# An SSM and mixture-of-experts kernel: GpSimd's skip, residual and low rows in other units, group 2's rows ahead of a weight split, group 3's projection in halves

## Chip, cores, metric

One NeuronCore of one Trainium2 chip. The time is the device time of one launch in microseconds (us); the profile is of one further execution.

## What is computed

The input `x` is 2 sequences of 2048 tokens of 256 numbers. First a state space layer, then a layer norm, then a mixture of experts, and a last layer norm; cut to its core:

```python
state = tanh(state @ A.T + x_t @ B.T)                 # 128 states, token after token
y  = states @ C.T + D * x + x
x1 = layernorm(x + layernorm(y) * gamma + beta)       # 256 numbers a token
scores = sigmoid(x1 @ router_weight.T)                # 8 experts in 2 groups of 4
# the better group (sum of its top two of scores + bias), in it the top 2 experts, weights normalised
routed = sum_e comb[t, e] * (silu(x1 @ w_gate[e]) * (x1 @ w_up[e])) @ w_down[e]
shared = (silu(x1 @ sw_gate) * (x1 @ sw_up)) @ sw_down
out = layernorm(x1 + routed + shared)
```

## The kernel before

**Data and stages.** The 4096 tokens lie as 32 tiles of 128 in `xres`; four tiles are a group, so there are 8 groups, 0 to 7. The scan runs all chunks of the sequences side by side in 64 steps; in the second 32 it leaves the states of one tile per step. Work on the first groups is put between those steps.

Every group goes through a *front*, each step on the engine that is named:

- GpSimd (`rows_in`): `skip` writes (D+1) * x into `xskip` (L1329), `residual` adds beta into `xres` (L1334), both 128x1024 in fp32.
- TensorE `project` (L385): states times C, eight matmuls into two PSUM banks, one for each half of two tiles; `c_done` counts the halves.
- VectorE `rows_sums` (L1009: PSUM plus `xskip`, a half each) and `row_moments` (L991 to L995), `scale_rows` (L1025), `sum_rows` (L1035), `sum_moments`: two layer norms. GpSimd takes the powers in `deviations1` (L1352, L1354) and `deviations2` (L1359 to L1365). ScalarE `normalise` (L710) writes the rows.
- ScalarE `high_rows` (L717) rounds the rows to fp16, and GpSimd `low_rows` (L1379) writes the rest as a second fp16 part; `note_tiles` (L1390) copies tile numbers.
- TensorE `turn_x2` (L396), ScalarE `keep_turned` (L724), TensorE `logits` (L403), ScalarE `scores` (a tanh, L733).
- VectorE `choose_group` (L1056 to L1072: nine instructions on 32 numbers a partition or fewer), TensorE `places` (L412 to L414), VectorE `sort_tiles` (L1135 to L1147), `choose_two` (L1086 to L1093), `weigh` (L1107 to L1119).
- TensorE `permute` (L418) with ScalarE `put` (L752), TensorE `turn_comb` (L438) with ScalarE `put_comb` (L761): tokens and weights sorted by expert group, at column offsets that VectorE casts to integers (L1147) and ScalarE reads (`offsets`).

**Passes and units.** The sorted tokens are taken in 10 passes, 0 to 9, of 2, 2, then six times 4, then 2, 2 tiles. A pass goes through 5 units (the shared expert, unit 0, and four routed ones), the last through 9: 54 units, n = 0 to 53. "Short" passes have 2 tiles, "wide" ones 4. A unit on TensorE is `up` (gate and up, L457), `spread` of the expert's weights (L467, which waits until the product before it is done), and two units later `down` (L480). ScalarE applies `silu` (L768) and rounds the product (`high`, L777); VectorE `inner` multiplies (L1155, or L1158 and L1162); GpSimd `low` (L1384) writes the product's low fp16 part, for which `down` waits. At a pass's end ScalarE `sums` and VectorE `close` (moments), GpSimd `deviations3`, ScalarE `finish` (L791), and GpSimd `send` (L1428: an indirect DMA for each tile).

**Order.** Every engine's queue is written out by hand and runs in order. In the loop over units each engine does its part of unit n and then the front steps that are due in it: `due(n, ahead, first)` gives the group whose position is `ahead` units on. So in a wide pass i the routing of group i + 1 and the rows of group i + 2 are under way: `choose_group` and `rows` in unit 0, `sort_tiles`, `scale_rows` and `sum_rows` in unit 1, `sum_moments` and `choose_two` in unit 2, `weigh` in unit 3. GpSimd's loop begins with

```python
for n, (i, j) in enumerate(UNITS):
    if n:
        low(n - 1, ...)
    g = due(n, EP, 2)                 # unit 0 of a wide pass
    if g is not None:
        low_rows(g, g % 3, main)
        note_tiles(g, main)
    ...                               # deviations1, plan, deviations2, watch, deviations3
    if 1 <= i <= G - 5 and j == 4:
        rows_in(i + 4)                # skip and residual of group i + 4
    if j in (0, 1) and i >= 2:
        send(i - 2, ...)              # half of pass i - 2's tiles
```

The weights are split into two fp16 parts by VectorE (`split`, L966 and L968, 128x2304): gate and up before the fronts, the down weights (`split(2)`) behind group 1's moments.

Of the kernel before, what the change touches and what calls it, by code (L numbers as in the profile page):

```python
# [20 lines left out]
def ssm_moe_kernel(nc, x, A, B, C, D, gamma, beta, router_weight, correction_bias,  # L21
# [20 lines left out]
    with ExitStack() as ctx:  # L42
# [181 lines left out]
        def ps_projected(g, half, sems):  # L224
            if sems is main and g == 2:
                return bank[half]
            return ps_misc[1 - half]
# [104 lines left out]
        def _(pe):  # L332
# [46 lines left out]
            def project(g, at, sems):  # L379

                for half in range(2):
                    if half and sems is main and g >= 3:
                        pe.wait_ge(main.th_done, g if g > 3 else 2)
# [140 lines left out]
            for i in range(L):  # L524
# [14 lines left out]
                if i == 24:  # L539
                    logits(0, main)  # L540
                if i == 27:
                    places(0)
                if i == 28:
                    pe.wait_ge(main.th_done, 1)
                    turn_x2(1, 1, main)
# [7 lines left out]
            project(3, 3 * T4, main)  # L553
# [53 lines left out]
            def front_late(n):  # L607
                g = due(n, EP + 2, 2)
# [87 lines left out]
        def _(act):  # L696
# [113 lines left out]
            for i in range(L):  # L810
# [6 lines left out]
                if i == 27:  # L817
                    high_rows(0, 0, main)
                if i == 25:
                    scores(0, main)  # L820
                if 23 <= i < 23 + T4:
                    normalise(1, 1, main, (i - 23,))
                if 28 <= i < 28 + T4:
                    at += offsets(0, (i - 28,))
                if i == 29:
                    keep_turned(1, main)

            put(0, 0, at)
# [87 lines left out]
        def _(dve):  # L916
# [80 lines left out]
            def rows_sums(g, par, sems):  # L997

                for half in range(2):
# [177 lines left out]
            for g in range(2):  # L1177
# [3 lines left out]
                sum_moments(g, g, main)  # L1181
            split(2)
            choose_group(0, main)
            sort_tiles(0)
            rows_sums(2, 2, main)
            choose_two(0, main)
            weigh(0, main)
            row_moments(2, 2, main)
            choose_group(1, main)
            scale_rows(2, 2, main)  # L1190
            rows_sums(3, 0, main)
            sort_tiles(1)

            for n, (i, j) in enumerate(UNITS):
# [28 lines left out]
                if n == 0:  # L1223
                    sum_moments(2, 2, main)
                if n == 2:
# [58 lines left out]
        def _(pool):  # L1284
# [52 lines left out]
            def rows_in(n):  # L1337
# [3 lines left out]
                skip(n)  # L1341
                pool.wait_ge(skip_done, (n + 1) * T4)
# [93 lines left out]
            note_tiles(0, main)  # L1436
            plan(0)
            watch(0)
            deviations1(2, 2, main)
# [3 lines left out]
            for n, (i, j) in enumerate(UNITS):  # L1443
                if n:
                    low(n - 1, n - 1, TILES[UNITS[n - 1][0]] * P, main)
                g = due(n, EP, 2)
                if g is not None:
                    low_rows(g, g % 3, main)
                    note_tiles(g, main)
# [4 lines left out]
                if g is not None:  # L1454
                    plan(g)
                g = due(n, 2 * EP - 2, 4)
# [11 lines left out]
                if j == 4 and i:  # L1468
                    deviations3(i - 1, (i - 1) % 2, TB[i - 1], TILES[i - 1], main)
                if 1 <= i <= G - 5 and j == 4:  # L1470
# [63 lines left out]
```

## Time and profile before

| what | value |
|---|---|
| median of 3 runs | 345.87 us (345.06 to 346.21) |
| the profiled execution | 347.44 us, span 345.7 us |
| TensorE matmul busy (PE) | 301.0 us, 87% of the span |
| VectorE busy (DVE) | 232.4 us, 67% |
| ScalarE busy (ACT) | 187.7 us, 54% |
| GpSimd busy (POOL) | 215.0 us, 62% |
| the chain that ended last, by engine | PE 38%, DVE 31%, issue 8%, POOL 7%, SP's queue 6%, ACT 5% |

The span is from the first to the last instruction of the profiled execution, and the rest of its time lies around it. Engine names in rows: PE is TensorE, DVE VectorE, ACT ScalarE, POOL GpSimd. A timeline row is: start and duration in us, engine, line, operation, what it writes and reads (by the buffers' names; several tensors share one, so that `low_rows` shows as `wg<-xskip,wg` and `low` as `h<-wu,h`), shape, how many of them the row merges, and in brackets the idle time of the engine just before and what ended it. A windows row has the window and its us, then busy us (instructions) of PE, of PE's weight loads, of DVE, ACT and POOL, then the granted TensorE clock as a share of full speed, the DMA share and GB/s.

### The profile page before, as it was taken

To read this page: it belongs to the slowest core of one execution; us is meant where nothing else is said; L and a number is where in the kernel's file an instruction comes from. 1 tells how busy PE (TensorE), PEld (TensorE's weight loads), DVE (VectorE), ACT (ScalarE), POOL (GpSimd) and SP (SyncE) were. 2 spreads that over 40 slices of the span, in tenths; PEclk is the share of its full clock that TensorE was granted. 3 is DMA by queue.
4 is the path that set the end of the run, shared out by engine and by line. 5 is a ranking of instruction groups with operands and counts; after the bars stand their busy time and mean duration, and the time that the engine had idled before them with its cause. 6 is when DMAs were issued, how large, how long until landed. Compare 5 with 4: busy or idle time off the path is not lost.

```text
span 345.7 us, 7383 instructions
## 1 busy us (share of the span) xinstructions
PE 301.0 (87%) x2255; PEld 228.7 (66%) x2255; DVE 232.4 (67%) x671; ACT 187.7 (54%) x442; POOL 215.0 (62%) x326
## 2 busy tenths in 40 slices
PE   5999999979878698798988999799999999998930
PEld 4998988878667465455655745476666656887820
DVE  2244979676998848995899599779936725363420
ACT  2465423545784593268358646756866772644430
POOL 8799013552545549567885986579777474776632
PEclk9999999985889999899999999999999999999985
DMA  6993000000000000000000010010001010011000
GB/s 190 339 335 121 0 3 0 0 2 0 2 2 2 0 2 1 33 0 2 15 19 1 2 43 20 0 34 32 0 17 48 2 47 15 28 37 63 30 8 32
DMA packets 6811, 13.20 MB, mean 38 GB/s; under 512 B 1000, under 2 KB 3568, under 8 KB 6768
## 3 DMA queue, kind: packets, MB, share of 16 engines
q1 hardware_dynamic: 5232, 8.47, 7.6%
q0 software_dynamic: 1536, 4.20, 3.4%
q8 instruction: 22, 0.36, 0.4%
q14 instruction: 21, 0.17, 0.2%
HBM read 8.47 MB, written 4.19 MB: 37 GB/s over the span
## 4 chain that ended last, share of the span: by engine, by line
PE 38%; DVE 31%; issue 8%; POOL 7%; SPq 6%; ACT 5%; DMA 2%; ACTq 1%; POOLq 0%; DVEq 0%
PE bank L457 14%; PE bank L480 8%; DVE st L991 5%; PE bank L403 4%; SPq L301 3%; DVE xskip L1035 3%; DVE xskip L1025 3%; PE bank L367 3%; DVE wd L1158 2%; DMA xres<-in_L_attn_x_dram 2%; PE bank L373 2%; POOL out_dram L1428 2%; DVE wu L1162 2%; DVE xskip L1009 2%; DVE more L1060 2%
## 5 line engine op out<-in xcount | busy, mean ns | idle before, releaser
L1384 POOL TENSOR_TENSOR h<-wu,h 128x512 f16<-128x512 f32 (+1 forms) x54 | 51.4, 953 | 50.9 <-ACT h L777 50.5
L480 PE MATMUL bank<-wd,h 128*128 (+1 forms) x504 | 65.2, 276 | 2.3 <-POOL h L1384 2.0
L457 PE MATMUL bank<-xT,wg 128*128 x324 | 64.6, 336 | 0.2 <-ACT wg L768 0.2
L457 PE MATMUL bank<-xT,wu 128*128 x324 | 63.4, 332 | 0.0
L768 ACT ACTIVATE wg<-bank,g_un 128x512 f32<-128x512 f32 (+1 forms) x54 | 31.9, 592 | 47.7 <-PE bank L457 47.5
L480 PEld LDWEIGHTS bank<-wd,h 128*128 128x128 f16 x504 | 47.8, 100 | 10.5 <-POOL h L1384 2.6
L1158 DVE SCALAR_TENSOR_TENSOR wd<-bank,u_un,wg 128x512 f32<-128x512 f32 (+1 forms) x44 | 27.2, 619 | 34.5 <-PE bank L457 17.8
L457 PEld LDWEIGHTS bank<-xT,wu 128*128 (+1 forms) x324 | 31.7, 98 | 23.0 <-issue 0.2
L457 PEld LDWEIGHTS bank<-xT,wg 128*128 (+1 forms) x324 | 31.3, 99 | 18.0 <-issue 1.1
L367 PE MATMUL bank<-xT,BT 128*128 128x128 f32 x256 | 41.4, 286 | 0.0
L752 ACT ACTIVATE xT<-bank 128x512 f32 (+1 forms) x64 | 33.8, 605 | 13.8 <-PE bank L418 9.4
L367 PEld LDWEIGHTS bank<-xT,BT 128*128 128x128 f32 x256 | 35.8, 202 | 0.1
L777 ACT ACTIVATE h<-wu 128x512 f16<-128x512 f32 (+1 forms) x54 | 28.6, 529 | 5.2 <-DVE wu L1162 4.5
L1162 DVE TENSOR_TENSOR wu<-bank,wd 128x512 f32<-128x512 f32 (+1 forms) x44 | 25.1, 570 | 1.5
L1379 POOL TENSOR_TENSOR wg<-xskip,wg 128x1024 f16<-128x1024 f32 x8 | 17.6, 2198 | 9.5 <-ACT wg L717 9.5
L991 DVE BATCH_NORM_STATS2 st<-xskip 128x6 f32<-128x256 f32 x64 | 22.4, 412 | 0.3
L1428 POOL DMA_INDIRECT out_dram<-z_odd,row_id x16 | 18.4, 1147 | 5.7 <-issue 3.2
L704 ACT ACTIVATE states<-bank 128x128 f32<-128x128 f32 x32 | 8.9, 277 | 22.2 <-PE bank L373 18.6
L1329 POOL TENSOR_TENSOR xskip<-xres,D_bc 128x1024 f32<-128x1024 f32 x8 | 18.9, 2358 | 1.6 <-PE bank L356 1.6
L710 ACT ACTIVATE xskip<-xskip,shift,rstd 128x256 f32<-128x256 f32 x32 | 17.2, 597 | 4.3 <-POOL shift L1365 4.3
L1334 POOL TENSOR_TENSOR xres<-xres,beta_bc 128x1024 f32<-128x1024 f32 x8 | 18.8, 2356 | 1.1
L704 ACT ACTIVATE run_state<-bank 128x128 f32<-128x128 f32 x31 | 8.6, 277 | 20.1 <-PE bank L373 20.1
(186 smaller groups left out, 568.2 us busy)
## 6 DMA issues: line engine op xcount, KB each, us to landing
xres<-in_L_attn_x_dram SPq DMA_DIRECT2D x7, 512.0 KB, 6.3
wd<-in_L_ffn_w_down_dram SPq DMA_DIRECT2D x1, 1024.0 KB, 6.7
xres<-in_L_attn_x_dram SPq DMA_DIRECT2D x2, 256.0 KB, 3.2
out_dram<-wd,row_id POOLq DMA_INDIRECT x16
out_dram<-z_odd,row_id POOLq DMA_INDIRECT x16
states<-in_L_attn_B_dram SPq DMA_DIRECT2D x1, 128.0 KB, 2.1
D_bc<-in_L_attn_D_dram SPq DMA_DIRECT2D x1, 128.0 KB, 5.0
beta_bc<-in_L_attn_beta_dram SPq DMA_DIRECT2D x1, 128.0 KB, 6.5
```

The source lines that it names most:

```text
L367: pe.matmul(ps_scan[s % 2][:, 0:P], BT[:, k, :], xT[:, k, tile, :], start=(k == 0), stop=False)
L457: last = pe.matmul(ps[:, 0:w], up_rows[which][pw][:, part], x2_sorted[:, k * 2 + px, bass.ds(col, w)], start=first, stop=(k == KT - 1 and ...
L480: last = pe.matmul(ps_y[t // 2][:, (t % 2) * DM:(t % 2 + 1) * DM], h16[:, m % 3, ph, t * P:(t + 1) * P], down_rows[pw][:, rows], start=(fi ...
L752: nc.scalar.activation(x2_sorted[:, :, bass.ds(where, P)], ps_rows(g, t)[:, :].rearrange("p (a c) -> p a c", a=2 * KT), ACT.Copy).then_inc ...
L768: nc.scalar.activation(sg[:, m % 2, 0:w], ps_g[:, 0:w], ACT.Silu, scale=g_un[:, 0:1]).then_inc(sems.silu_done, 1)
L777: nc.scalar.activation(h16[:, m % 3, 0, 0:w], h[:, m % 2, 0:w], ACT.Copy).then_inc(sems.h_high, 1)
L991: nc.vector.bn_stats(st[:, st_k, t, :], src(t)).then_inc(st_sem, 1)
L1158: nc.vector.scalar_tensor_tensor(gu[:, m % 2, 0:w], ps_u[m % 2][:, 0:w], u_un[:, 1:2], sg[:, m % 2, 0:w], ALU.mult, ALU.mult).then_inc(sem ...
L1162: nc.vector.tensor_tensor(h[:, m % 2, 0:w], ps_comb[:, 0:w], gu[:, m % 2, 0:w], ALU.mult).then_inc(sems.h_done, 1)
L1329: nc.gpsimd.tensor_tensor(xskip[:, n * T4:(n + 1) * T4, :], xres[:, n * T4:(n + 1) * T4, :], D_bc[:, :].unsqueeze(1).to_broadcast([P, T4, ...
L1384: nc.gpsimd.tensor_tensor(h16[:, m % 3, 1, 0:w], h[:, m % 2, 0:w], h16[:, m % 3, 0, 0:w], ALU.subtract).then_inc(sems.h_low, 1)
L1428: nc.gpsimd.indirect_dma_start(out_rows, bass.IndirectOffsetOnAxis(row_id[:, ring, t:t + 1], 0), z2s[par][:, t, :], None, bounds_check=N - ...
```

## The change

It changes the order of instructions only; none is added or removed, and one PSUM bank is another.

- The scan: `logits(0)` goes from step 24 to 23, `places(0)` from 27 to 28, `turn_x2(1)` from 28 to 27; on ScalarE `high_rows(0)` from 27 to 21, `scores(0)` from 25 to 23, `keep_turned(1)` from 29 to 28, the offsets of group 0 from steps 28 to 31 to steps 30, 31 and behind the scan.
- VectorE does `rows(2)` (sums and moments) ahead of `split(2)`, and `scale_rows(2)` ahead of `choose_group(1)`.
- Group 3's projection leaves its place ahead of the first unit: its halves go behind units 0 and 1, both into bank `ps_y[1]`, which short passes don't use; the second waits for the sum of the first. VectorE sums them in units 1 and 2.
- GpSimd: `deviations1(2)` ahead of `plan(0)`; in the loop `low_rows` and `note_tiles` go behind the sends of the same unit; the skip of group i + 4 goes from unit 4 to unit 2 of passes 1 to 3, ahead of `deviations2`, and the residual stays in unit 4.

```diff
@@ ps_projected
+            if sems is main and g == 3:
+                return ps_y[1]
@@ TensorE
-            def project(g, at, sems):
-                for half in range(2):
-                    if half and sems is main and g >= 3:
-                        pe.wait_ge(main.th_done, g if g > 3 else 2)
+            def project(g, at, sems, halves=range(2)):
+                for half in halves:
+                    if half and sems is main and g == 3:
+                        pe.wait_ge(main.y1_done, 2 * g + 1)
+                    if half and sems is main and g > 3:
+                        pe.wait_ge(main.th_done, g)
...
-                if i == 24:
+                if i == 23:
                     logits(0, main)
+                if i == 28:
+                    places(0)
                 if i == 27:
-                    places(0)
-                if i == 28:
                     pe.wait_ge(main.th_done, 1)
                     turn_x2(1, 1, main)
...
             turn_comb(0)
-            project(3, 3 * T4, main)
             taken_at[0] = take(0)
             places(1)
...
             def front_late(n):
+                if n in (0, 1):
+                    project(3, 3 * T4, main, (n,))
@@ ScalarE
-                if i == 27:
+                if i == 21:
                     high_rows(0, 0, main)
-                if i == 25:
+                if i == 23:
                     scores(0, main)
...
-                if 28 <= i < 28 + T4:
-                    at += offsets(0, (i - 28,))
-                if i == 29:
+                if 30 <= i < 30 + T4:
+                    at += offsets(0, (i - 30,))
+                if i == 28:
                     keep_turned(1, main)
+            at += offsets(0, range(len(at), T4))
@@ VectorE
+            rows(2, 2, main)
             split(2)
             choose_group(0, main)
             sort_tiles(0)
-            rows_sums(2, 2, main)
             choose_two(0, main)
             weigh(0, main)
-            row_moments(2, 2, main)
+            scale_rows(2, 2, main)
             choose_group(1, main)
-            scale_rows(2, 2, main)
-            rows_sums(3, 0, main)
             sort_tiles(1)
...
+                if n == 1:
+                    rows_sums(3, 0, main, (0,))
+                if n == 2:
+                    rows_sums(3, 0, main, (1,))
@@ GpSimd
+            deviations1(2, 2, main)
             plan(0)
             watch(0)
-            deviations1(2, 2, main)
...
                     low(n - 1, n - 1, TILES[UNITS[n - 1][0]] * P, main)
-                g = due(n, EP, 2)
-                if g is not None:
-                    low_rows(g, g % 3, main)
-                    note_tiles(g, main)
...
                     plan(g)
+                if 1 <= i <= G - 5 and j == 2:
+                    pool.wait_ge(x_in[i + 4], 16)
+                    skip(i + 4)
...
                 if 1 <= i <= G - 5 and j == 4:
-                    rows_in(i + 4)
+                    rows_kept(i + 4)
                 if j in (0, 1) and i >= 2:
...
                     send(i - 2, i % 2, (i - 2) % 3, TB[i - 2], TILES[i - 2], main, range(j * half, (j + 1) * half))
+                g = due(n, EP, 2)
+                if g is not None:
+                    low_rows(g, g % 3, main)
+                    note_tiles(g, main)
```

## Rows read from the trace of the kernel before

**Rows 1.** Windows view, passes 2 to 5: busy us (instructions), clock, DMA.

```profile
130.00:163.10 33.10, 28.07 (x189) 17.53 (x189) 27.66 (x72) 17.58 (x38) 23.11 (x32) 0.95 0.03 9
163.10:193.80 30.70, 27.90 (x201) 18.07 (x200) 26.07 (x75) 18.39 (x39) 24.14 (x31) 1.00 0.03 10
193.80:225.30 31.50, 28.07 (x201) 18.15 (x201) 26.84 (x76) 19.56 (x41) 22.40 (x34) 1.00 0.05 18
225.30:253.20 27.90, 27.28 (x201) 18.24 (x200) 23.23 (x75) 19.14 (x41) 21.02 (x32) 1.00 0.06 20
```

**Rows 2.** Timeline, VectorE, pass 2: start, us, engine, line, operation, count, idle before.

```profile
131.95 1.70 DVE L1056 TENSOR_SCALAR score<-th 128x32 f32<-128x32 f32 x1 [1.16 <-ACT th L733]
...
134.31 2.04 DVE L1060 TENSOR_TENSOR more<-choice 128x16 f32<-128x16 f32 x1
...
139.24 1.29 DVE L1009 TENSOR_TENSOR xskip<-bank,xskip 128x512 f32<-128x512 f32 x2
```

**Rows 3.** Timeline, GpSimd (POOL), the same stretch.

```profile
131.25 2.35 POOL L1334 TENSOR_TENSOR xres<-xres,beta_bc 128x1024 f32<-128x1024 f32 x1
...
134.19 2.13 POOL L1379 TENSOR_TENSOR wg<-xskip,wg 128x1024 f16<-128x1024 f32 x1
```

**Rows 4.** Timeline, VectorE, the chain undisturbed, in pass 4, in pass 5.

```profile
84.74 0.18 DVE L1056 TENSOR_SCALAR score<-th 128x32 f32<-128x32 f32 x1 [2.14 <-ACT th L733]
...
86.24 1.67 DVE L1025 SCALAR_TENSOR_TENSOR xskip<-xskip,mv,gamma_bc 128x256 f32<-128x256 f32 x4
...
195.84 0.78 DVE L1056 TENSOR_SCALAR score<-th 128x32 f32<-128x32 f32 x1 [1.15 <-ACT th L733]
...
200.79 1.29 DVE L1009 TENSOR_TENSOR xskip<-bank,xskip 128x512 f32<-128x512 f32 x2
...
227.30 1.17 DVE L1056 TENSOR_SCALAR score<-th 128x32 f32<-128x32 f32 x1 [1.15 <-ACT th L733]
...
229.82 1.29 DVE L1009 TENSOR_TENSOR xskip<-bank,xskip 128x512 f32<-128x512 f32 x2
```

**Rows 5.** Timeline, VectorE, from the split to the first unit.

```profile
63.80 2.62 DVE L968 SCALAR_TENSOR_TENSOR wd<-wd,wscale 128x2304 f16<-128x2304 f32 x1
69.78 0.18 DVE L1056 TENSOR_SCALAR score<-th 128x32 f32<-128x32 f32 x1 [3.37 <-ACT th L733]
...
72.49 0.21 DVE L1135 TENSOR_TENSOR_SCAN zeros_f<-ones_row,zeros_f,bank 1x4 f32<-1x4 f32 x1 [1.24 <-PE bank L414]
...
73.80 2.09 DVE L1147 CAST zeros_i<-zeros_f 1x4 int32<-1x4 f32 x1
...
80.79 1.40 DVE L991 BATCH_NORM_STATS2 st<-xskip 128x6 f32<-128x256 f32 x4
...
90.71 0.46 DVE L1155 SCALAR_TENSOR_TENSOR wu<-bank,u_un,wg 128x256 f32<-128x256 f32 x1
```

**Rows 6.** Timeline, GpSimd, the first low_rows.

```profile
73.21 2.65 POOL L1379 TENSOR_TENSOR wg<-xskip,wg 128x1024 f16<-128x1024 f32 x1 [5.51 <-ACT wg L717]
```

**Rows 7.** Timeline, ScalarE (ACT), group 1's first normalisation.

```profile
67.74 0.60 ACT L710 ACTIVATE xskip<-xskip,shift,rstd 128x256 f32<-128x256 f32 x1 [2.12 <-POOL shift L1365]
```

**Rows 8.** Timeline, TensorE (PE), the projection ahead of the first unit.

```profile
84.71 3.73 PE L385 MATMUL bank<-CT,states 128*128 128x256 f32 x8
```

**Rows 9.** Timeline, GpSimd, short pass 1, pass 4, pass 5.

```profile
120.12 0.67 POOL L1384 TENSOR_TENSOR h<-wu,h 128x256 f16<-128x256 f32 x1 [1.69 <-ACT h L777]
...
214.58 0.20 POOL L1359 TENSOR_TENSOR rstd<-mv,eps 128x4 f32<-128x4 f32 x1 [2.88 <-DVE mv L995]
...
228.74 1.13 POOL L1428 DMA_INDIRECT out_dram<-z_odd,row_id  x1 [0.15 <-ACT z_odd L791]
```

**Rows 10.** Timeline, TensorE, the wait for the weights in pass 5.

```profile
247.63 0.40 PE L438 MATMUL bank<-perm,comb 128*128 128x128 f16 x4 [0.53 <-DVE comb L1119]
```

**Rows 11.** Timeline, VectorE, weigh in pass 1, scaling in pass 4.

```profile
121.13 0.19 DVE L1110 SCALAR_TENSOR_TENSOR kept<-rank,score 128x32 f32<-128x32 f32 x1
...
206.59 3.21 DVE L1025 SCALAR_TENSOR_TENSOR xskip<-xskip,mv,gamma_bc 128x256 f32<-128x256 f32 x4
```

More of the change, by code:

```diff
@@ L995, in stats, with rows_sums @@
                     nc.vector.bn_aggr(to[:, t, :], st[:, st_k, t, :]).then_inc(mv_sem, 1)
-            def rows_sums(g, par, sems):
-                for half in range(2):
+            def rows_sums(g, par, sems, halves=range(2)):
+                for half in halves:
                     dve.wait_ge(sems.c_done, g * 2 + half + 1)
@@ L1341, in rows_in, with rows_kept @@
                 skip(n)
+                rows_kept(n)
+            def rows_kept(n):
                 pool.wait_ge(skip_done, (n + 1) * T4)
```

## The prediction, on record before the change was run

> **What bounds the kernel now.** I read the windows view first, cut where VectorE notes a new wide pass (four tiles). TensorE is busy 28 us in each of passes 2, 3 and 4 and 27.3 us in pass 5, with the same work in all four; but pass 5 lasts 27.9 us and the others 33.1, 30.7 and 31.5 [rows 1]. So TensorE's work is a floor of about 27.3 us, and passes 2 to 4 stand 3 to 6 us above it.
>
> Next the VectorE timeline of the slowest pass. The routing chain `choose_group(3)` starts at 131.95, and the sums that follow it at 139.24: 7.3 us for nine tiny instructions, single ones of 1.70 and 2.04 us [rows 2]. The GpSimd timeline says why [rows 3]: a residual runs from 131.25 to 133.60, and L1056 ends at 133.65; `low_rows` runs from 134.19 to 136.32, and L1060 ends at 136.35. A VectorE instruction on SBUF that starts inside a large GpSimd instruction ends when that one ends. Undisturbed the same chain takes 84.74 to 86.24, that is 1.5 us; in pass 4 it takes 4.95 us (pass 3 is like it, 0.3 us shorter), in pass 5, which has no skip and residual ahead of it, 2.5 us [rows 4].
>
> The Trainium skill (SBUF — State Buffer, "Who interferes with whom") calls this an exclusive lock: VectorE and GpSimd share one pair of ports, held for a whole instruction. The rows above agree to 0.1 us.
>
> Last, the stretch from the end of the scan to the first unit. VectorE holds the split's second half from 63.80 to 66.42 and spends 2.09 us on a 1x4 cast at 73.80 [rows 5], inside `low_rows(0)` at 73.21 [rows 6]; ScalarE, which runs the scan's tanh in the same queue, waits for that cast's result, and before it 2.12 us for GpSimd's deviations, held up by the split [rows 7]. The projection of group 3 then takes 3.73 us ahead of the first unit [rows 8], whose VectorE work begins at 90.71 [rows 5].
>
> **The change, part by part.** T is the instant at which the tanh of a group's logits ends.
>
> *Group 2's rows ahead of the split, the scan's steps in another order.* I follow VectorE from `choose_group(0)` to the first unit. It starts about 1 us later: the rows (two sums of 0.65, moments 1.41, aggregates 0.4: 3.1 us) push the split into the 3.37 us in which VectorE waits [rows 5], and `low_rows(0)`, which `high_rows(0)` at step 21 now releases near the split, can hold that for up to its own 2.65 us [rows 6]. I take half. From there on the chain loses: the cast's lockout (2.09 - 0.15 = 1.95), group 2's sums (1.3), its moments (1.85), group 3's sums (1.3) and part of the 2.14 us wait for the tanh of group 1, which the scan, no longer standing 2.12 us and at the cast, brings earlier [rows 4, 5, 7]: 1.1, half. It gains the wait for `places(1)`, now with nothing beside it (group 0's is 1.24, I take 0.7 [rows 5]), and a lockout by `low_rows(1)`, which falls between `choose_group(1)` and `sort_tiles(1)` (0 to 2.13; half, 1.1). +1.0 - 1.95 - 1.3 - 1.85 - 1.3 - 1.1 + 0.7 + 1.1 = -4.7 us: the first unit near 86.0. Bounds: both lockouts in full and no earlier tanh, -1.2; none of them, -8. TensorE no longer has the projection's 3.73 us ahead of the unit, so it isn't what comes last.
>
> *Group 3 in halves.* TensorE's halves (under 1.9 us each) go behind units 0 and 1, where it waits for VectorE; the two sums go into VectorE's units 1 and 2. VectorE has no break there and carries `weigh(1)`, for which TensorE waits. One of the two stands ahead of it: +0.65 us (0 to 1.3).
>
> *The skip at unit 2, the residual alone at unit 4, `low_rows` behind the sends.* The residual now ends a skip earlier, about 1 us before T, and `low` near T. A send waits for `finish`, which ScalarE runs behind the tanh; its DMA takes 1.13 us [rows 9]. So `low_rows` starts some 2 us after T in passes 2 and 3 (one DMA) and 3.3 us in passes 4 and 5 (two), when `choose_group` (1.5 us) is over and VectorE is at sums, moments and the unit's products, which read PSUM or one operand: L1009 keeps 0.65 us apiece [rows 2]. So `choose_group` falls to 1.5 us: 5.8, 3.2, 3.45 and 1.0 us less in passes 2 to 5. TensorE's floor caps what comes of it.
>
> What is late next is the skip's new place. Behind it on GpSimd stand the second deviations and the next unit's `low`; ScalarE's normalisation waits for the first, TensorE's down projection for the second. A skip has the residual's shape and its 2.35 us [rows 3]. Two rows bound its price. In pass 4 GpSimd is idle 2.88 us, from 211.70 to the second deviations at 214.58 [rows 9]: there it would fit, price 0. But what ends that idle time is the moments, and right behind them on VectorE stands `choose_two`; that comes 18.8 us behind T now and, 3.45 us earlier, at T+15.3, while GpSimd is free near T+15.9 or, with less in its way, some 2 us before. So the skip meets `choose_two` or `weigh` in passes 2 and 3: 0 to 2.35 us of VectorE. TensorE waits for `weigh`'s result (already 0.53 us in pass 5 [rows 10]). I take 1.6 us: 27.4 + 1.6 = 29.0 us each (27.5 to 30). In pass 1 the skip starts when `low(6)` ends, 120.79 [rows 9], `weigh(2)`, for whose end TensorE waits, reads two SBUF operands from 121.13 on [rows 11]: 120.79 + 2.35 - 121.13 = +2.0 us (0 to 3). Passes 4 and 5 have no skip; what remains is `low` among the scaling: four of 3.21 us in pass 4 [rows 11] against 1.67 undisturbed [rows 4], so up to 1.5 us. I take 27.9 and 27.6 (27.3 to 28.8).
>
> The Trainium skill (same page and section) says that issue order decides who blocks, and that the other blocks fully. That speaks against this part: a skip is issued ahead of the routing on which TensorE waits next. By it each of the three skips costs 2.35 us, 7.05 in place of 5.2, and the sum below would be -9.9. L1060 agrees that the loser blocks fully; who comes first at the new place no row shows.
>
> **Sum.** First unit -4.7, halves +0.6, pass 1 +2.0, pass 2 from 33.1 to 29.0 = -4.1, pass 3 -1.7, pass 4 -3.6, pass 5 -0.3: -11.8 us. Passes 6 to 9 keep their work. The profiled execution took 347.44 us (span 345.7, the rest around it), 1.6 us above the median of the runs, 345.87; the difference carries over: 334.1 us.
>
> **Rivals.**
> 1. *Down to TensorE's floor.* The skips fall into GpSimd's idle time, pass 1 loses nothing, passes 2 to 5 take 27.4 or 27.5: 123.2 - 109.8 = -13.4, with -4.1 early -17.5: 328.4 us. For it: pass 5 is within 0.6 us of its floor. Against: the idle slot ends where `choose_two` starts.
> 2. *The skip locks out in full.* 2.35 us three times (+1.9), and each pushes `low` back, so that TensorE's down projection waits another 1 us (+3): -6.9, 339.0 us. For it: pass 1's rows. Against: VectorE can come first.
> 3. *Slower: the large operations only change their victim.* `low_rows` behind the sends reaches `sort_tiles` and the scaling, for which the permutation waits. It decides if it starts later than T+4.5: a DMA issue stretched by 1.2 us does it. Price per pass 2.13, and 1.55 for the `low` behind it, in four passes, plus three skips: 14.7 + 7.05 = 21.8, against 13.45 of stalls removed and 4.1 early: +4.2, 350 us. Against: the second DMA should end by T+3.3.
> 4. *It doesn't do what it says.* GpSimd is a microsecond late everywhere, residual and `low` still run into `choose_group`, and the skips cost as forecast: the passes give nothing, pass 1's skip takes 2.0 and one other 1.6 of the early 4.1: 345.4 us.
>
> **How the numbers follow.** Forecast 0.57, rival 1 0.20, rival 2 0.15, rival 3 0.05, rival 4 0.03. The forecast's own bounds are 330 to 338; the range reaches to rivals 1 and 2 and takes in the bounds of the first part: 327.5 to 341. A measurement of this kernel can tell 0.3% (1 us) from no change: faster 0.92, same 0.03, slower 0.05.
>
> **What would show it.** Right: L1060 at 0.2 us and 1.5 us for `choose_group` in passes 2 to 5, with `low_rows` behind the DMAs; windows of 28 to 29 us; the first L1155 near 86; ScalarE's stand of 2.12 us gone; a skip beside `choose_two` (L1086 to L1093) or `weigh` (L1110), with one of those at 1 to 2.4 us. Wrong: TensorE waiting for `low` (L1384) at its down projections; L1144 or L1025 stretched by `low_rows`; a first unit that starts no earlier, because `choose_group(0)` starts later.

## The result, and the profile after

The changed kernel takes 335.52 us (median of 4 runs, 332.56 to 337.0) against 345.65 us of the kernel before on the same chip: ratio 0.968, 95% interval [0.965, 0.972]. The forecast was 334.1 us, in a range of 327.5 to 341. Its profiled execution took 337.0 us (span 335.3), the longest of the four.

The line numbers of the changed kernel are 4 to 12 higher than before: `choose_group` L1063 to L1079, `rows_sums` L1016, `scale_rows` L1032, `sum_rows` L1042, `choose_two` L1093 to L1100, `weigh` L1114 to L1126, `skip` L1338, `residual` L1343, `low_rows` L1391, `low` L1396, `send` L1440; on TensorE `project` L389, `turn_comb` L442.

First the windows view of passes 2 to 5, cut as [rows 1]:

```profile
127.30:155.80 28.50, 26.49 (x194) 17.20 (x190) 22.84 (x71) 17.76 (x38) 21.87 (x33) 1.00 0.03 11
155.80:186.60 30.80, 28.94 (x201) 19.50 (x201) 24.08 (x75) 18.32 (x39) 23.32 (x32) 0.94 0.03 10
186.60:215.60 29.00, 27.54 (x201) 18.36 (x201) 23.66 (x76) 19.45 (x41) 19.36 (x32) 1.00 0.06 20
215.60:243.50 27.90, 27.33 (x201) 18.31 (x200) 22.53 (x76) 19.18 (x41) 20.47 (x32) 1.00 0.06 20
```

Pass 2 lost 4.8 us and pass 4 2.5, pass 5 nothing; pass 3 is as long as before. From one cast of the row numbers, with which VectorE opens a pass, to the next (us):

| | first unit | pass 0 | pass 1 | pass 2 | pass 3 | pass 4 | pass 5 | sum to pass 6 |
|---|---|---|---|---|---|---|---|---|
| before | 90.64 | 21.79 | 17.50 | 33.15 | 30.73 | 31.47 | 27.95 | 253.23 |
| after | 85.80 | 22.17 | 19.48 | 28.37 | 30.81 | 28.96 | 27.91 | 243.50 |
| difference | -4.84 | +0.38 | +1.98 | -4.78 | +0.08 | -2.51 | -0.04 | -9.73 |
| forecast | -4.7 | +0.6 | +2.0 | -4.1 | -1.7 | -3.6 | -0.3 | -11.8 |

*What went as forecast.* The VectorE timeline of pass 2, then the GpSimd timeline beside it (columns as in [rows 2, 3]):

```profile
129.47 0.18 DVE L1063 TENSOR_SCALAR score<-th 128x32 f32<-128x32 f32 x1 [1.16 <-ACT th L739]
129.92 0.17 DVE L1067 TENSOR_TENSOR more<-choice 128x16 f32<-128x16 f32 x1
130.97 1.36 DVE L1016 TENSOR_TENSOR xskip<-bank,xskip 128x512 f32<-128x512 f32 x2
```

```profile
124.98 2.35 POOL L1343 TENSOR_TENSOR xres<-xres,beta_bc 128x1024 f32<-128x1024 f32 x1
...
130.94 1.26 POOL L1440 DMA_INDIRECT out_dram<-wd,row_id  x1 [2.98 <-ACT wd L797]
132.24 2.14 POOL L1391 TENSOR_TENSOR wg<-xskip,wg 128x1024 f16<-128x1024 f32 x1
...
142.23 2.35 POOL L1338 TENSOR_TENSOR xskip<-xres,D_bc 128x1024 f32<-128x1024 f32 x1
145.14 0.20 POOL L1371 TENSOR_TENSOR rstd<-mv,eps 128x4 f32<-128x4 f32 x1 [0.56 <-DVE mv L1002]
```

The 7.3 us of [rows 2] are 1.5 us (129.47 to 130.97), and the instruction that took 2.04 us takes 0.17. The residual is over 2.1 us before `choose_group` starts, and `low_rows` starts 1.3 us after `choose_group` is done, behind a send. This skip cost nothing: it ends at 144.58, and GpSimd then still waits 0.56 us for the moments; without it, in experiment 5, the pass takes 28.38 us against 28.37.

*What the large operations hit next.* VectorE in passes 1, 2, 3 and 4; the first and third row stand in a skip (GpSimd, below), the second and fourth hold `low`:

```profile
116.69 2.01 DVE L1117 SCALAR_TENSOR_TENSOR kept<-rank,score 128x32 f32<-128x32 f32 x1
...
137.06 2.90 DVE L1032 SCALAR_TENSOR_TENSOR xskip<-xskip,mv,gamma_bc 128x256 f32<-128x256 f32 x3
...
172.36 2.18 DVE L1093 TENSOR_TENSOR choice<-choice,mask 128x32 f32<-128x32 f32 x1
...
198.48 3.20 DVE L1042 SCALAR_TENSOR_TENSOR xskip<-xskip,rstd,xres 128x256 f32<-128x256 f32 x4
```

```profile
116.30 2.35 POOL L1338 TENSOR_TENSOR xskip<-xres,D_bc 128x1024 f32<-128x1024 f32 x1
...
138.50 1.17 POOL L1396 TENSOR_TENSOR h<-wu,h 128x512 f16<-128x512 f32 x1
...
172.13 2.34 POOL L1338 TENSOR_TENSOR xskip<-xres,D_bc 128x1024 f32<-128x1024 f32 x1
...
198.67 1.14 POOL L1440 DMA_INDIRECT out_dram<-wd,row_id  x1 [0.31 <-issue]
199.80 1.19 POOL L1396 TENSOR_TENSOR h<-wu,h 128x512 f16<-128x512 f32 x1
```

L1117 takes 0.19 us where nothing is beside it, L1093 0.17. All four stand ahead of `weigh` or in it, and TensorE waits for `weigh` at the end of the pass. Its wait there in pass 1 of the kernel before, then in passes 1 to 5 of the changed one (timelines of TensorE):

```profile
122.69 0.40 PE L438 MATMUL bank<-perm,comb 128*128 128x128 f16 x4 [0.32 <-DVE comb L1119]
```

```profile
120.25 0.40 PE L442 MATMUL bank<-perm,comb 128*128 128x128 f16 x4 [2.33 <-DVE comb L1126]
...
150.29 0.40 PE L442 MATMUL bank<-perm,comb 128*128 128x128 f16 x4 [1.38 <-DVE comb L1126]
...
179.68 0.40 PE L442 MATMUL bank<-perm,comb 128*128 128x128 f16 x4 [1.39 <-DVE comb L1126]
...
210.05 0.40 PE L442 MATMUL bank<-perm,comb 128*128 128x128 f16 x4 [1.39 <-DVE comb L1126]
...
237.91 0.40 PE L442 MATMUL bank<-perm,comb 128*128 128x128 f16 x4 [0.49 <-DVE comb L1126]
```

In pass 1 the wait grew by 2.0 us. In passes 2 to 4 it was 1.38 to 1.39 us before too. So 1.39 says that VectorE is the later of the two at the end of a pass, but not by how much: TensorE's matmul just ahead waits for VectorE's last product, `weigh` follows that product without a break, and the remaining wait is then the same however late VectorE is. What a pass lost is read from its length.

*The early part.* VectorE from the split to the first unit, against [rows 5]:

```profile
65.60 2.17 DVE L973 TENSOR_SCALAR wd<-wd,wscale 128x2304 f16<-128x2304 f32 x1
67.81 2.62 DVE L975 SCALAR_TENSOR_TENSOR wd<-wd,wscale 128x2304 f16<-128x2304 f32 x1
70.34 0.17 DVE L1063 TENSOR_SCALAR score<-th 128x32 f32<-128x32 f32 x1
...
73.87 0.21 DVE L1142 TENSOR_TENSOR_SCAN zeros_f<-ones_row,zeros_f,bank 1x4 f32<-1x4 f32 x1 [2.08 <-PE bank L418]
...
75.19 0.15 DVE L1154 CAST zeros_i<-zeros_f 1x4 int32<-1x4 f32 x1
...
80.63 0.18 DVE L1063 TENSOR_SCALAR score<-th 128x32 f32<-128x32 f32 x1
...
83.00 2.08 DVE L1147 TENSOR_TENSOR pos<-pos 128x4 f32<-128x4 f32 x1
...
85.87 0.46 DVE L1162 SCALAR_TENSOR_TENSOR wu<-bank,u_un,wg 128x256 f32<-128x256 f32 x1
```

The chain starts 0.6 us later, its cast takes 0.15 us, the second `choose_group` no longer waits for its tanh, and `low_rows(1)` holds L1147: the first unit's work at 85.87 (forecast 86.0).

*Pass 3.* The windows view, 4 us each, behind the wait of 1.39 us:

```profile
176.00:180.00 4.00, 2.14 (x13) 0.89 (x12) 3.69 (x13) 3.17 (x6) 1.75 (x5) 1.00 0.00 0
180.00:184.00 4.00, 4.00 (x24) 3.25 (x22) 2.64 (x10) 2.46 (x10) 3.84 (x8) 0.57 0.02 4
```

The granted clock falls to 0.57, close to the lower of its two levels, 1.2 of 2.4 GHz, right behind a slice in which TensorE was busy for 2.14 of 4 us. Four profiles below whose passes 2 to 4 run the same code (the loop's edits alone, split first, projection whole, steps as before) have a pass 3 of 29.4 us at a clock of 1.00, two more (offsets early, offsets late) one of 30.8 with the same 0.57 in the 4 us behind this wait. So 1.4 us of this profile's pass 3 are the clock's, and the change is worth 1.3 us in pass 3 without it.

### The profile page after: what moved, and what is told of

Same layout as the page of the kernel before. It is cut to its first block, busy times and chain, and to the rows that moved or that the text cites. A ratio compares the mean times of both kernels' runs of the same rounds, so it can differ in the third digit from the quotient of the medians.

```text
span 335.3 us, 7382 instructions
## 1 busy us (share of the span) xinstructions
PE 295.4 (88%) x2255; PEld 225.1 (67%) x2255; DVE 225.5 (67%) x671; ACT 187.6 (56%) x442; POOL 212.9 (64%) x326
## 4 chain that ended last, share of the span: by engine, by line
PE 48%; DVE 24%; POOL 8%; issue 6%; SPq 6%; ACT 3%; DMA 3%; ACTq 0%; POOLq 0%; DVEq 0%
PE bank L461 16%; PE bank L484 9%; PE bank L369 6%; PE bank L375 4%; PE bank L407 4%; POOL out_dram L1440 4%; SPq L303 3%; PE bank L389 3%; DVE xskip L1042 3%; DMA xres<-in_L_attn_x_dram 3%; DVE wd L1165 3%; DVE wu L1169 2%; PE bank L400 2%; DVE xskip L1032 2%; POOL h L1396 2%
## 5 line engine op out<-in xcount | busy, mean ns | idle before, releaser
L1396 POOL TENSOR_TENSOR h<-wu,h 128x512 f16<-128x512 f32 (+1 forms) x54 | 53.1, 986 | 45.8 <-ACT h L783 45.6
L484 PE MATMUL bank<-wd,h 128*128 (+1 forms) x504 | 64.6, 274 | 2.3 <-POOL h L1396 2.0
L484 PEld LDWEIGHTS bank<-wd,h 128*128 128x128 f16 x504 | 47.4, 99 | 10.4 <-POOL h L1396 2.6
L1165 DVE SCALAR_TENSOR_TENSOR wd<-bank,u_un,wg 128x512 f32<-128x512 f32 (+1 forms) x44 | 27.3, 621 | 31.3 <-PE bank L461 17.3
L758 ACT ACTIVATE xT<-bank 128x512 f32 (+1 forms) x64 | 33.8, 610 | 11.3 <-PE bank L422 10.0
L1440 POOL DMA_INDIRECT out_dram<-wd,row_id x16 | 17.5, 1093 | 11.2 <-ACT wd L797 8.2
L1440 POOL DMA_INDIRECT out_dram<-z_odd,row_id x16 | 17.8, 1113 | 9.9 <-ACT z_odd L797 6.9
L1391 POOL TENSOR_TENSOR wg<-xskip,wg 128x1024 f16<-128x1024 f32 x8 | 17.1, 2138 | 4.6 <-ACT wg L723 4.5
L1338 POOL TENSOR_TENSOR xskip<-xres,D_bc 128x1024 f32<-128x1024 f32 x8 | 18.9, 2356 | 1.1 <-PE bank L358 1.1
L1343 POOL TENSOR_TENSOR xres<-xres,beta_bc 128x1024 f32<-128x1024 f32 x8 | 18.8, 2356 | 0.7
```

Source lines behind the costliest of these rows:

```text
L484: last = pe.matmul(ps_y[t // 2][:, (t % 2) * DM:(t % 2 + 1) * DM], h16[:, m % 3, ph, t * P:(t + 1) * P], down_rows[pw][:, rows], start=(fi ...
L758: nc.scalar.activation(x2_sorted[:, :, bass.ds(where, P)], ps_rows(g, t)[:, :].rearrange("p (a c) -> p a c", a=2 * KT), ACT.Copy).then_inc ...
L1165: nc.vector.scalar_tensor_tensor(gu[:, m % 2, 0:w], ps_u[m % 2][:, 0:w], u_un[:, 1:2], sg[:, m % 2, 0:w], ALU.mult, ALU.mult).then_inc(sem ...
L1338: nc.gpsimd.tensor_tensor(xskip[:, n * T4:(n + 1) * T4, :], xres[:, n * T4:(n + 1) * T4, :], D_bc[:, :].unsqueeze(1).to_broadcast([P, T4, ...
L1396: nc.gpsimd.tensor_tensor(h16[:, m % 3, 1, 0:w], h[:, m % 2, 0:w], h16[:, m % 3, 0, 0:w], ALU.subtract).then_inc(sems.h_low, 1)
L1440: nc.gpsimd.indirect_dma_start(out_rows, bass.IndirectOffsetOnAxis(row_id[:, ring, t:t + 1], 0), z2s[par][:, t, :], None, bounds_check=N - ...
```

## The experiments

Each was timed in five rounds; ratios are to the kernel before beside it (median 346.46 us for the first three and the skips in the scan, 346.79 for the next four, 346.99 for the last three).

**1. The skip back in unit 4.**

```diff
-                if 1 <= i <= G - 5 and j == 2:
-                    pool.wait_ge(x_in[i + 4], 16)
-                    skip(i + 4)
...
                 if 1 <= i <= G - 5 and j == 4:
-                    rows_kept(i + 4)
+                    rows_in(i + 4)
```

> The changed kernel with one part undone: the skip of group i + 4 goes back from unit 2 to unit 4, ahead of the residual. Theory (a large GpSimd operation holds whatever VectorE instruction on two SBUF operands or on a copy mode falls into it): the residual ends 2.35 us later again, about 1 to 2 us behind T, and low behind it, so choose_group of passes 2 to 4 takes 3.5 to 4.5 us in place of 1.5; but no skip stands in weigh(2) of pass 1 (-2.0 us) nor in choose_two of pass 3 (-2.0). Pass 1 19.5 to 17.5 us, pass 2 28.4 to about 30, pass 3 30.8 to about 30, pass 4 29.0 to about 30.5: 335 to 337 us, hardly a difference from the changed kernel. Rival (moving the skip is what the gain rests on): passes 2 to 4 go back to 31 to 33 us and the time to 342 us or more.

339.06 us, ratio 0.980 [0.977, 0.982]: between the two, and 3.5 us worse than the changed kernel. VectorE and GpSimd in pass 2 show why:

```profile
125.88 1.78 DVE L1063 TENSOR_SCALAR score<-th 128x32 f32<-128x32 f32 x1 [1.16 <-ACT th L739]
...
128.76 4.38 DVE L1072 TENSOR_TENSOR across<-more 128x8 f32<-128x8 f32 x1
...
133.66 1.29 DVE L1016 TENSOR_TENSOR xskip<-bank,xskip 128x512 f32<-128x512 f32 x2
```

```profile
125.27 2.36 POOL L1343 TENSOR_TENSOR xres<-xres,beta_bc 128x1024 f32<-128x1024 f32 x1
...
128.44 1.26 POOL L1440 DMA_INDIRECT out_dram<-wd,row_id  x1 [0.19 <-issue]
129.73 2.14 POOL L1391 TENSOR_TENSOR wg<-xskip,wg 128x1024 f16<-128x1024 f32 x1
131.80 0.21 POOL L1402 COPY comb<-tile_no 128x4 f16<-128x4 f16 x1
131.95 1.16 POOL L1396 TENSOR_TENSOR h<-wu,h 128x512 f16<-128x512 f32 x1
```

With a late residual GpSimd has no break between the send, `low_rows`, `note_tiles` and `low`, and one VectorE instruction of 0.16 us is held through all of them, to 133.14. `choose_group` takes 7.8 us, more than before. Passes 2 and 3 take 33.63 and 31.66 us; in pass 4, where two issues stand ahead of `low_rows`, it runs behind `choose_group`, and the pass takes 28.45. The theory hadn't counted the stall of the first two.

**2. `low_rows` back at the head of the unit.**

```diff
                     low(n - 1, n - 1, TILES[UNITS[n - 1][0]] * P, main)
+                g = due(n, EP, 2)
+                if g is not None:
+                    low_rows(g, g % 3, main)
+                    note_tiles(g, main)
```

(and taken out behind the sends)

> The changed kernel with one part undone: low_rows goes back ahead of everything else in its unit, behind low. Theory: low ends near T, low_rows runs from T to T+2.1 and choose_group, which begins at T+0.05, loses most of that: 2.5 to 3.5 us in place of 1.5 in passes 2 to 5. TensorE has no slack for it in passes 2 to 4: +1 to +2 us each, +0.5 in pass 5; 338 to 341 us. Rival (the residual's move alone frees choose_group, low_rows does not matter): within 1 us of the changed kernel's 335.5.

334.95 us, ratio 0.967 [0.964, 0.971]: no difference from the changed kernel, as the rival had it. In this profile `choose_group` takes 2.1 to 2.8 us in passes 2 to 5 in place of 1.5, and nobody waits for it. The chain of the changed kernel in pass 3 says why (start, us, what):

```profile
157.58 1.33 PE bank L484 x12
158.90 1.73 PE bank L389 x8
160.63 2.29 PE bank L461 x11
163.32 0.76 DVE wd L1165
...
172.44 2.11 DVE choice L1093
```

Up to 163 us the chain is TensorE's own work, from the logits over `down` (L484) to the projection (L389, ended at 160.63, which the second sum needs) and `up`; `choose_group` (157.84 to 159.37) isn't on it and has slack of about 1 us. From the units' products on it is VectorE's, up to `weigh`.

**3. The early part alone** (the loop's edits undone, with both diffs above) and **4. the loop's edits alone** (put into the kernel before):

```diff
-                g = due(n, EP, 2)
-                if g is not None:
-                    low_rows(g, g % 3, main)
-                    note_tiles(g, main)
...
+                if 1 <= i <= G - 5 and j == 2:
+                    pool.wait_ge(x_in[i + 4], 16)
+                    skip(i + 4)
...
-                    rows_in(i + 4)
+                    rows_kept(i + 4)
...
                     send(i - 2, ...)
+                g = due(n, EP, 2)
+                if g is not None:
+                    low_rows(g, g % 3, main)
+                    note_tiles(g, main)
```

> The kernel before with only the part ahead of the first unit and group 3's halves; GpSimd's loop as before. Theory (the two parts add up): the first VectorE work of unit 0 starts at 85.9 as in the changed kernel, +0.4 for the halves, the wide passes as before at 33, 31 and 31.5 us: 345.65 - 4.5 = 341.2 us. Rival (the early part is lost again in the wide passes, because the routing of groups 3 and 4 ends the wait there): 345 us.

> The kernel before with only GpSimd's loop of the changed one: skip at unit 2, residual alone at unit 4, low_rows behind the sends. Theory (the two parts add up, since each ends in a place where TensorE has no slack): the first unit starts as before (VectorE 90.7), the passes as in the changed kernel, pass 1 2.0 us longer, pass 2 28.4, pass 3 29 to 31, pass 4 29.0: 345.9 - 5.3 to 7 = 339 to 341 us. Rival (the skip's lockouts eat the loop's part whole): 345 us.

341.51 us, ratio 0.985 [0.983, 0.988], that is -5.1 us; and 340.34 us, ratio 0.982 [0.978, 0.986], that is -6.2 us. The sum, -11.3, is the change's -10.1 to -10.9 within the intervals: the two parts add. Experiments 1 to 3 and the changed kernel are all four cases of two edits: with both undone 341.5 us, with `low_rows` moved alone 339.1 (-2.5), with the skip moved alone 335.0 (-6.6), with both 335.5. Pass 4 shows why they don't add: it is 31.43 us with neither, 28.45 with `low_rows` alone, 28.27 with the skip alone, 28.96 with both (27.92 in two other profiles of the same loop, see experiment 5).

**5. The skips of groups 5 to 7 in the scan**, where GpSimd waits for the front anyway.

```diff
+            pool.wait_ge(back_made, 1)
+            for n in (5, 6):
+                pool.wait_ge(x_in[n], 16)
+                skip(n)
             deviations1(0, 0, main)
+            pool.wait_ge(x_in[7], 16)
+            pool.wait_ge(main.z1_done, T4)
+            skip(7)
             deviations2(0, 0, main)
...
-                if 1 <= i <= G - 5 and j == 2:
-                    pool.wait_ge(x_in[i + 4], 16)
-                    skip(i + 4)
```

> The changed kernel with the three skips taken out of the loop over units: those of groups 5 and 6 run in GpSimd's idle time behind the second weight split (about 43.4 to 48.2 us), that of group 7 behind group 0's second moments' inputs (about 52.4 to 54.8), where VectorE reads PSUM or one operand. Theory (the skip's price in the loop is the lockout of weigh(2) and choose_two): pass 1 2.0 us less, pass 3 2.0 us less and, if TensorE's drop of the granted clock there (0.50 from 182 to 184 us) follows from its wait for weigh, another 1.5; pass 2 the same: 330 to 332 us. Rival (skips cost nothing, pass 3 is long by its clock alone): 335 us in the median.

330.13 us, ratio 0.952 [0.949, 0.954], 5.4 us less than the changed kernel. The windows view, then GpSimd in pass 4:

```profile
126.50:154.90 28.40, 26.38 (x189) 17.09 (x189) 22.85 (x72) 17.65 (x38) 20.65 (x32) 1.00 0.03 11
154.90:182.50 27.60, 27.30 (x201) 18.27 (x200) 22.09 (x75) 17.93 (x39) 20.15 (x30) 1.00 0.04 12
182.50:210.40 27.90, 27.31 (x201) 18.31 (x201) 22.54 (x75) 19.17 (x41) 21.20 (x33) 1.00 0.06 20
```

```profile
194.55 2.38 POOL L1440 DMA_INDIRECT out_dram<-wd,row_id  x1 [0.30 <-issue]
```

Pass 1 is 17.58 us again (19.48 with the skip), pass 3 27.6 at full clock, pass 4 27.9: there the send's second issue runs from 194.55 to 196.93 and `low` starts behind it, when VectorE's `sum_rows` (194.41, 1.65 us) is over.

Not all of that is the skips'. From the changed kernel's profile to this one pass 1 gives 1.9 us, pass 3 3.2 (1.4 of it the clock's) and pass 4 1.0, and the first unit takes 1.0 back. But pass 4 takes 27.92 us in the profiles of experiments 4 and 9 too, where the skips stand at unit 2. In these, here and in experiment 11 the second issue starts 0.13 to 0.14 us behind `sum_rows` and takes 2.37 or 2.38 us; in the changed kernel and in experiments 6, 7, 8 and 10 it starts 0.18 or 0.19 us behind, takes 1.13 or 1.14, and `low` falls into `sum_rows`: 28.94 to 28.96 us. The two outcomes lie 0.05 us apart in that start; what moves it was not tried. What the profiles show as the skips' own price is about 3.7 us, in passes 1 and 3.

**6. The split ahead of group 2's rows**, as before, and **7. group 3's projection whole** ahead of the first unit, as before.

```diff
-            rows(2, 2, main)
             split(2)
+            rows(2, 2, main)
```

```diff
             turn_comb(0)
+            project(3, 3 * T4, main)
...
             choose_group(1, main)
+            rows_sums(3, 0, main)
             sort_tiles(1)
```

(7 also takes the halves out of the first units)

> The changed kernel with one edit undone: split(2) again ahead of group 2's sums and moments. Theory (what comes last ahead of the first unit is VectorE's chain and low_rows(1), not the deviations of group 1): the split then runs undisturbed from 62.6 to 66.6, the rows to 69.7, choose_group(0) starts near 70, as in the changed kernel (70.34), and GpSimd's deviations for group 1 come near 68, when the tanh of the logits is only just done: first unit within 0.5 us of 85.9, the time within 1 us of 335.5. Rival (the edit is what removed ScalarE's 2.12 us stand, and the scan pays it again): first unit near 88, 337.5 us or more.

> The changed kernel with one edit undone: group 3's projection whole ahead of places(1), its sums ahead of sort_tiles(1). Theory (the halves move work out of a place that has slack by now): TensorE's 1.9 us lie in its 2.53 us wait for choose_group(1), VectorE's 1.3 us beside low_rows(1), which holds sort_tiles(1) until 85.06 anyway; first unit within 0.7 us of 85.9, and units 1 and 2 get back 0.4 to 1.3 us: 334.5 to 336 us, no worse than the changed kernel. Rival (the projection ahead of the first unit costs its 1.9 to 3.7 us there): 337.5 to 339 us.

335.48 us, ratio 0.968 [0.964, 0.973], and 335.86 us, ratio 0.969 [0.966, 0.972]: undone alone, neither edit is worth anything that can be measured.

**8. The steps of the scan as before**, all else as changed.

```diff
-                if i == 21:
+                if i == 27:
                     high_rows(0, 0, main)
-                if i == 23:
+                if i == 25:
                     scores(0, main)
-                if 30 <= i < 30 + T4:
-                    at += offsets(0, (i - 30,))
+                if 28 <= i < 28 + T4:
+                    at += offsets(0, (i - 28,))
```

(and TensorE's three steps and `keep_turned(1)`)

> The changed kernel with one edit undone: the scan's steps (logits, places, turn, high_rows, scores, offsets) as in the kernel before. Theory (high_rows(0) at step 27 puts low_rows(0) on the cast of the offsets again, and ScalarE waits for that cast at step 28, with three steps of the scan behind it): the 1x4 cast takes 1.5 to 2.1 us again, the scan ends 2 to 3 us later, the first unit starts near 88: 337.5 to 338.5 us. Rival (the order of the steps does not matter once the rows are ahead of the split): 335.5 us.

338.19 us, ratio 0.976 [0.972, 0.979], 2.7 us worse than the changed kernel, with the first unit at 89.12. The cast of group 0's offsets is not held here (0.16 us at 74.91), so that lockout isn't what the order of the steps removes. Which of the steps counts, two more runs tell apart.

**9. The offsets read early**, all else as changed, and **10. the offsets read late**, the other steps as before.

```diff
-                if 30 <= i < 30 + T4:
-                    at += offsets(0, (i - 30,))
+                if 28 <= i < 28 + T4:
+                    at += offsets(0, (i - 28,))
...
-            at += offsets(0, range(len(at), T4))
```

(in 10 the offsets stay as changed, with `logits(0)`, `places(0)`, `turn_x2(1)`, `high_rows(0)`, `scores(0)` and `keep_turned(1)` at their old steps)

> The changed kernel, with ScalarE reading the column offsets of group 0 at steps 28 to 31 of the scan, as before, and every other step of the scan as changed. Open from the run with all the scan's steps as before (338.2 us, 2.7 us slower than the changed kernel): which of the steps is worth that. Theory A, the offsets: read at step 28 they stop ScalarE's queue, and with it the scan's tanh, until VectorE's cast of the offsets is done; with all the steps as before ScalarE stood 3.68 us for that cast and VectorE then 3.46 us for the tanh of group 1's logits, although the cast itself came at 74.9, as in the changed kernel (75.2). So 337.5 to 338.5 us here, and a wait of 2 us or more of ScalarE for the cast. Theory B, high_rows(0) at step 21, which moves the first low_rows off the cast and the chain: 335 to 336 us, as the changed kernel.

> The changed kernel with the scan's steps as before (high_rows(0) at 27, scores(0) at 25, logits(0) at 24, places(0) at 27, turn_x2(1) at 28, keep_turned(1) at 29), but the offsets of group 0 read at steps 30, 31 and behind the scan, as changed. Theory A (the offsets' read is what counts): 335 to 336.3 us, and no wait of ScalarE for the cast of more than 1 us inside the scan. Theory B (the other steps count): 337.5 to 338.5 us.

337.68 us, ratio 0.976 [0.973, 0.978], and 335.61 us, ratio 0.968 [0.966, 0.970]: it is the offsets. ScalarE in the kernel before and with the offsets read early, then VectorE of the latter (whose line numbers are one less here than in the changed kernel):

```profile
76.70 0.28 ACT L704 ACTIVATE states<-bank 128x128 f32<-128x128 f32 x1 [3.40 <-DVE zeros_i L1147]
```

```profile
74.65 1.09 ACT L730 ACTIVATE wu<-bank 128x512 f32<-128x512 f32 x2 [2.63 <-DVE zeros_i L1153]
```

```profile
81.48 0.18 DVE L1062 TENSOR_SCALAR score<-th 128x32 f32<-128x32 f32 x1 [2.32 <-ACT th L739]
```

Reading an offset at step 28 stops ScalarE's queue for 2.63 us (9) to 3.68 us (8), 3.40 before, until the cast is done; the scan's tanh stand behind it, and VectorE waits for the logits that follow the scan. With the offsets read late (10) ScalarE waits for no cast, VectorE not for that tanh, and the first unit's work is at 84.57, against 86.75 with them read early (9).

**11. `low` behind `sum_rows`**, on top of 5: in passes 2 to 5 the `low` of unit 1 waits until VectorE has done `sum_rows`.

```diff
+                if 2 <= i <= 5 and j == 2:
+                    pool.wait_ge(main.z1_done, (i + 3) * T4)
                 if n:
                     low(n - 1, n - 1, TILES[UNITS[n - 1][0]] * P, main)
```

> The kernel with the skips of groups 5 to 7 in the scan (330.1 us), and in passes 2 to 5 the low of unit 1 waits until VectorE's sum_rows of the same pass are done, so that it no longer runs inside VectorE's scaling, which took 3.29 us in pass 2 with it and 1.65 us in pass 4 of the changed kernel without. Theory: where low ran inside the scaling, TensorE waited 1.39 us for weigh at the end of the pass, and pass 2 took 28.4 us against 27.6 to 27.9 of the passes behind it; so pass 2 falls to 27.7, the others stay: 329 to 329.7 us. Rival: low now ends some 2 us later and TensorE's down projection waits for it instead: 330 to 331.5 us.

328.53 us (328.27 to 329.39), ratio 0.947 [0.946, 0.949], the fastest of all. Windows of passes 2 and 3, then VectorE's scaling in pass 2:

```profile
125.50:152.20 26.70, 25.98 (x189) 17.08 (x189) 21.21 (x71) 17.34 (x38) 19.96 (x32) 1.00 0.03 11
152.20:179.90 27.70, 27.40 (x202) 18.39 (x201) 22.09 (x76) 18.04 (x39) 18.51 (x31) 1.00 0.04 12
```

```profile
135.12 1.65 DVE L1032 SCALAR_TENSOR_TENSOR xskip<-xskip,mv,gamma_bc 128x256 f32<-128x256 f32 x4
```

Pass 2 lost another 1.6 us (28.38 to 26.75), more than expected because it has less work than the passes behind it (point 7 below): L1032 takes 1.65 us in place of 3.29, TensorE waits 0.69 us for `weigh` in place of 1.39, and its down projection doesn't wait for the later `low`.

## Why the prediction was right, and where its terms were off

The mechanism held. VectorE's small instructions were held by GpSimd's large ones, `choose_group` is 1.5 us with those moved, and the skip's new place gave part of it back. That the sum came within 1.4 us is in part luck: several terms missed, both ways, and two stretches come out in one of two ways with the same code (pass 3's clock, 1.4 us; pass 4's second send, 1.0 us). Rivals 3 and 4 didn't come: `low_rows` reached neither the sorting nor the scaling in passes 2 to 5, and GpSimd's order held.

1. *First unit, -4.7.* -5.1 by the times of experiment 3. The -4.84 of the two profiles alone would prove less: the first unit's work starts at 84.65 to 86.32 in four profiles with the same changed early part (the changed kernel, experiments 1 to 3), and at 90.71 or 88.51 with the early part as before (the kernel before, experiment 4). The 84.65 and the 88.51 had a granted clock of 1.00 from 65 to 75 us, the others one of 0.77 to 0.89 there. The size was right and the working partly not. The prediction put 1.95 us on the cast's lockout and about 4.5 on sums and moments that leave the chain, and 1.1 on an earlier tanh. Experiments 8 to 10 give 2.2 to 2.7 us to the offsets' read alone, which the prediction named as a wait of ScalarE but priced only through the 2.14 us tanh wait of [rows 4]. Experiment 6 shows that the rows ahead of the split, undone alone, save nothing. The remaining 2.4 us or so belong to the other edits of that part (the scaling ahead of `choose_group(1)`, sums and moments off the chain); which of them was not tried.
2. *Halves, +0.6.* +0.38, and by experiment 7 no difference.
3. *Pass 1, +2.0.* +1.98: L1117 held 2.01 us, and TensorE's wait behind it 2.33 us in place of 0.32.
4. *Pass 2, 29.0.* 28.37. The skip was priced at 1.6 us and cost nothing; `low` in the scaling, priced only in passes 4 and 5, cost 1.6 (experiment 11). The size is luck: another operation than forecast cost the 1.6, on a floor that was lower (7).
5. *Pass 3, 29.0.* This is the term that was off: 30.81 in this profile, 29.4 without the fall of the clock. The skip held `choose_two` for 2.18 us, nearly in full as rival 2 said, and cost the pass 1.8 (29.4 us against 27.63 in experiment 5), where the prediction took 1.6; what it lacked is the clock. (It read `choose_two` at 18.8 us behind T; in pass 4 of the kernel before that is 18.6.)
6. *Pass 4, 27.9.* 28.96: `low` fell into `sum_rows` (3.20 us in place of 1.65), and TensorE's wait for `weigh` is 1.39 us, against 0.50 in experiment 9, where it didn't. The prediction named the cause with up to 1.5 us and took 0.5; its 27.9 is what the same loop takes when the second send goes the other way (experiment 5).
7. *The floor of 27.3.* For pass 2 it was too high, because the work isn't the same in all four: [rows 1] has 189 matmuls there against 201. The first two `down` in pass 2 are those of the last units of short pass 1, with 6 matmuls each in place of 12 (changed kernel, at 129.06 and 134.33), and 12 matmuls of `down` take 1.33 us in the chain above. So its floor is about 26.0 us: 25.98 busy in experiment 11, which did the pass in 26.75. That its busy time was 28.07 us in [rows 1] is in part the clock of 0.95; with the same loop at 1.00 it is 26.91 (experiment 3), in a pass that isn't shorter (33.30 us). Pass 3 in 27.6 and passes 4 and 5 in 27.9 lie at 27.3 to 27.4 of busy time.
8. *`low_rows` behind the sends* and the skip's move were both counted into `choose_group`'s gain. The skip's alone gives all of it: 6.6 us with `low_rows` where it was, 3.5 with it moved, both net of what the skips cost in their new place (about 3.7 us by the profiles of experiment 5). `low_rows`' move shortens `choose_group` by another 0.6 to 1.3 us and moves no time (experiment 2), because TensorE's own work up to the projection ends later.

The span lost 10.4 us against the 11.8 of the sum. Pass 3 took 1.8 us more than forecast (1.4 of it the clock's), pass 4 1.1, pass 5 0.3; the first unit, the halves and pass 2 gave 1.0 more, and the passes behind pass 5 0.7.

The Trainium skill's rule (SBUF — State Buffer, "Who interferes with whom"), by which issue order decides who blocks and the other blocks fully, put each skip, as the prediction applied it, at its whole 2.35 us. Two of the three agree (instructions held 2.01 and 2.18 us); the third, in pass 2, fell beside VectorE's products and moments, which were not held: four moments took 1.39 us inside it, against the 1.40 of [rows 5]. The prediction's own sentence, that a VectorE instruction on SBUF which starts inside a large GpSimd instruction ends when that one ends, was thus too wide.

## What to carry to other kernels

When a long GpSimd operation is taken out of VectorE's way, look for the place where both engines' chains have slack, and price what stands there: here moving the three skips by two units was worth 3.5 to 6.6 us, and moving them into the scan 5.4 us more. Before a held instruction is counted as a gain, follow the chain of waits through it: `choose_group` could be 1 us longer for nothing, while `sum_rows` 1.6 us longer cost its pass a whole microsecond. An engine whose queue reads a register from another engine's result stands there with all that is queued behind: 2 us came from reading four offsets two steps later.

## What the runs showed of the hardware

- A held VectorE instruction isn't let in between GpSimd operations that follow each other without a break: 4.38 us through an indirect DMA's issue, `low_rows`, a small copy and `low` (experiment 1).
- It goes the other way too: in pass 3 of the changed kernel a `low` that starts at 167.45, inside VectorE's scaling, takes 2.90 us in place of 1.17, while the scaling and `sum_rows` keep 1.66 us each. A DMA issue beside `sum_rows` took 2.37 to 2.38 us or 1.13 to 1.14, by whether it started 0.13 to 0.14 or 0.18 to 0.19 us behind it (experiment 5).
- TensorE's clock fell behind the same waits, 0.5 and 1.4 us, in some profiles and not in others of the same passes (pass 3 of 29.4 or 30.8 us). Pass 1 with the skip shows it as well: 19.4 to 19.6 us in six profiles, 20.5 at a mean clock of 0.92 in experiments 6 and 9. What decides it was not tried.
